# A graph network's gathered rows summed column by column, and handed on in groups of four

## The reference

```
x = x + L0(h)      # per edge: h[src] @ w[type], summed by target
x = x + L1(h)      # three times: mean of the neighbours' rows @ Wl + h @ Wr + b, relu between
x = x + L2(h)      # sums of h_src and of h_src * h_dst by target, @ weight1 and @ weight2, scaled by degrees
x = x + L3(h)      # two graph attentions: scores per edge, softmax by target, weighted sum
```

## Time and profile before

| | us |
|---|---|
| median of 3 runs | 6555.59 |
| span of the profiled execution | 8635.1 |
| PE, DVE, POOL busy in it | 4016.2, 4326.1, 4305.3 |
| layer0: from the first gather to the patch's gather | 731 (3108 to 3839) |
| layer1, layer2, layer3 likewise | 744, 698, 678 |
| att1: from its first gather to its last | 728 (6012 to 6740) |
| granted TensorE clock, mean of the span | 0.650 of full |

### The profile page before, as it was taken

The page is one execution under the profiler, slowest core; times in us unless marked ns, Lnnn a source line. Parts: engine busy times, 40 slices in busy tenths (PEclk is TensorE's granted clock), DMA queues, the critical chain, the costliest instruction groups (busy, mean ns, idle before and its releaser), DMA issues. The chain is left out here.

```text
span 8635.1 us, 76490 instructions
## 1 busy us (share of the span) xinstructions
PE 4016.2 (47%) x19708; PEld 2671.9 (31%) x19708; DVE 4326.1 (50%) x14882; ACT 2282.2 (26%) x5999; POOL 4305.3 (50%) x4026
## 2 busy tenths in 40 slices
PE   1111158312888825654563664342465476567000
PEld 0000034101555514443442443332344355233000
DVE  3010069301999944434432553565244698677553
ACT  0000000001777621110110333354111133799000
POOL 5777720575000046546555674774555100888577
PEclk8555589655999955555555555555666666798555
DMA  1111100000222222222222343343122144555222
GB/s 42 47 46 47 47 19 0 21 1 5 103 113 107 99 70 79 69 73 64 69 68 63 112 128 112 94 139 112 44 68 68 77 161 163 125 146 138 76 82 77
DMA packets 413612, 684.96 MB, mean 79 GB/s; under 512 B 283685, under 2 KB 290444, under 8 KB 407978
## 3 DMA queue, kind: packets, MB, share of 16 engines
q1 hardware_dynamic: 282410, 542.14, 17.7%
q0 software_dynamic: 130944, 140.05, 7.5%
HBM read 310.94 MB, written 373.78 MB: 79 GB/s over the span
## 5 line engine op out<-in xcount | busy, mean ns | idle before, releaser
L711 POOL DMA_INDIRECT G<-states,srcq x1568 | 1678.9, 1071 | 851.1 <-issue 479.5
L1133 DVE TENSOR_TENSOR_SCAN R<-same,R,G 128x28 f32<-128x28 f32 x4480 | 883.8, 265 | 622.1 <-issue 499.9
L1793 PE MATMUL PS<-ident,HH 128*128 128x128 f32 x2357 | 529.8, 376 | 1257.4 <-ACT AT L2063 373.2
L2063 ACT COPY AT<-PS 128x512 f32<-128x512 f32 (+1 forms) x494 | 283.7, 581 | 2467.3 <-remote 1375.1
L1793 PEld LDWEIGHTS PS<-ident,HH 128*128 128x128 f32 x2357 | 402.8, 205 | 1332.9 <-issue 409.9
L711 POOL DMA_INDIRECT EE<-node_info,srcq x392 | 394.4, 1006 | 545.0 <-DMA node_info<-XC 415.7
L1701 PE MATMUL PS<-R 128*128 128x392 f16 x784 | 283.0, 361 | 673.2 <-remote 375.7
L711 POOL DMA_INDIRECT G<-states,srci x392 | 406.7, 1038 | 321.0 <-ACT HH L2161 199.1
L1808 PEld LDWEIGHTS PS<-WD,AT 128*128 128x128 f32 x2358 | 505.8, 316 | 183.0 <-issue 182.7
L1808 PE MATMUL PS<-WD,AT 128*128 128x64 f32 x2358 | 560.6, 416 | 0.0
L824 POOL DMA_INDIRECT out_nodes<-O,dstq x392 | 430.9, 1099 | 188.2 <-issue 123.3
(11 more groups left out here) (412 smaller groups left out, 10157.6 us busy)
## 6 DMA issues: line engine op xcount, KB each, us to landing
states<-O SPq DMA_DIRECT2D x70, 896.0 KB, 3.6
HH<-states SPq DMA_DIRECT2D x56, 896.0 KB
total<-R SPq DMA_DIRECT2D x56, 896.0 KB
XB<-resid SPq DMA_DIRECT2D x42, 896.0 KB
states<-HH SPq DMA_DIRECT2D x28, 896.0 KB, 3.9
G<-states,srcq POOLq DMA_INDIRECT x1568
resid<-XB SPq DMA_DIRECT2D x28, 896.0 KB
xl_of_src<-O SPq DMA_DIRECT2D x14, 1792.0 KB
```

The source lines that it names most:

```text
L711: return pool.indirect_dma_start(to, None, table_, bass.IndirectOffsetOnAxis(ap=idx, axis=0), bounds_check=bound, oob_is_err=False).then_i ...
L1133: last = dve.tensor_tensor_scan(out=out_[:, order, f], data0=flags[:, order], data1=in_[:, order, f], initial=initial[:, f:f + 1], op0=ALU ...
L1793: last = pe.transpose(PS[:, 4 + k, q * P:(q + 1) * P], HH[:, b, (g * G4 + q) * D2:(g * G4 + q + 1) * D2], ident[:])
L2063: act.copy(AT[:, k, 0:n * P], PS[:, 4 + k, 0:n * P]).then_inc(s_copied, 1)
```

## The change

In the four `LAYERS` passes the 64 scans of a chunk are replaced by 28 steps of `scalar_tensor_tensor`, each over the 64 features of one column: column j = column j-1 times the flag `same` plus the gathered column j. Every step waits for the one before. After each four columns the operand of that group is made and `s_ready` is incremented, 7 times a chunk instead of once. The gathers signal one semaphore for each group and buffer (`s_g[b][g]`), and DVE waits for a group at a time. PE's `turn` waits for its own group. In `layer0` and `layer1` the one-hots and their matmuls move ahead of the chunk's rows and products. In `att1` ACT copies the left halves group by group, each copy one group ahead of the products, and PE waits for a group's left halves. A function `first_operands` replaces `operands` in the patch.

```diff
-                def gathered(i, it, b):
+                def rows_of(i, it, b):
                     step.reset()
                     dve.wait_ge(s_tot[b], before[layer, "tot"] + 16 * (it + 1))
                     step(dve.memset(col(SCR), 0.0))
-                    dve.wait_ge(s_g[b], before[layer, "gath"] + 16 * C * (it + 1))
-                    if k == 3:
-                        step(tt(cut(G[:, b, :]), cut(G[:, b, :]), over(rs_src[:, bass.ds(i * C, C)], D), ALU.mult))
-                    scans(cut(R[:, b, 0:CD]), cut(G[:, b, :]), same[:, bass.ds(i * C, C)], R[:, 1 - b, CD - D:CD], D).then_inc(s_scan, 1)
...
+                    for g in range(GROUPS):
+                        dve.wait_ge(s_g[b][g], before[layer, "gath"] + 16 * G4 * (it + 1))
+                        if k == 3:
+                            some = cut(G[:, b, g * G4 * D:(g + 1) * G4 * D])
+                            step(tt(some, some, over(rs_src[:, bass.ds(i * C + g * G4, G4)], D), ALU.mult))
+                        for j in range(g * G4, (g + 1) * G4):
+                            row_before = R[:, b, (j - 1) * D:j * D] if j else R[:, 1 - b, CD - D:CD]
+                            row = dve.scalar_tensor_tensor(out=R[:, b, j * D:(j + 1) * D], in0=row_before, scalar=same[:, bass.ds(i * C + j, 1)],
+                                                           in1=G[:, b, j * D:(j + 1) * D], op0=ALU.mult, op1=ALU.add)
+                            if j < C - 1:
+                                step(row)
+                        if g == GROUPS - 1:
+                            row.then_inc(s_scan, 1)
+                            dve.wait_ge(s_scan, before[layer, "scan"] + 1 + i)
+                        if g == 0:
+                            if k == 3:
+                                dve.wait_ge(s_rscaled, i + 1)
+                            else:
+                                dve.wait_ge(s_ld[b], before[layer, "ld"] + 16 * (it + 1))
+                            step(dve.memset(col(SCR), 0.0))
+                        operands(k, i, b, g).then_inc(s_ready, 1)
...
                     def turn(i, it, b):
-                        gathered(i, it, b)
-                        state(i, it, b)
+                        step.reset()
                         source_hots(i)
+                        rows_of(i, it, b)
...
-                pe.wait_ge(s_ready, before[phase, "ready"] + 1 + i)
+                if phase in LAYERS:
+                    pe.wait_ge(s_ready, before[phase, "ready"] + GROUPS * i + g + 1)
...
+                if phase == "att1":
+                    pe.wait_ge(s_left, GROUPS * i + g + 1)
...
             def scores1(i, it, b):
-                act.wait_ge(s_g[b], before["att1", "gath"] + 16 * C * (it + 1))
-                act.copy(cut(HH[:, b, :], D2)[:, :, 0:D], cut(G[:, b, :])).then_inc(s_left, 1)
-                put_scores(i, it, b)
+                def left(g):
+                    act.wait_ge(s_g[b][g], before["att1", "gath"] + 16 * G4 * (it + 1))
+                    some = slice(g * G4, (g + 1) * G4)
+                    act.copy(cut(HH[:, b, :], D2)[:, some, 0:D], cut(G[:, b, :])[:, some]).then_inc(s_left, 1)
```

## The result

The changed kernel takes 6359.17 us (median of 4 runs, 6354.62 to 6363.26) against 6554.74 us before (4 runs, 6538.55 to 6563.34): a ratio of 0.9706, 95% interval 0.9691 to 0.9720. It is 196 us faster.

What follows compares the result with a forecast made beforehand. POOL's gathers, about 1.30 us each, were taken to bound every pass. Terms -48 (layer0, layer1), -12 (layer2), +7 (layer3) and -12 (att1) sum to -65, so 6555.6 becomes 6490 us, range 6420 to 6600.

Steps and rivals of the forecast that it cites:

- The reading of the disturbed profile: All passes: the plain run has gathers at about 1.30 us; POOL's 338.8 us of waits for scans are no gain.
- Rival (b): Between chunks: POOL's waits for the scans exist in the plain run too; -300 us at most, so 6270; chance 0.12.
- The step that failed: Every pass: 14 x 36.4 us of gathers plus what follows the last gather, everything else moving beside them.
- Rival (d): Columns beside gathers: steps 0.73 us apart, hidden in layer0 to layer2, layer3 +166 us, 6650 in all; chance 0.15.
- Ends of layer0 and layer1: Behind the last gather: 40.3 us becomes 14.5 with nothing uncovered; 24 taken for each layer, -48 us together.
- Layer2: End of layer2: the front of the tail shortens from 16.3 to 4.2 us, the rest stays; -12 us.
- Layer3: New loop through DVE and ACT of 38.5 us a chunk against 36.4 of gathers; +7 us, bounds -15 to +62.
- att1: Start of the first attention: first products go at about 6047 instead of 6059.5; -12 us, bounds -12 to +14.
- The chained steps: DVE's column steps: 0.22 us of work plus a 0.14 us gap for a register or address instruction.
- (a): Gaps between chained steps vanish: layer3 gives -15 us instead of +7, ends another -5; 6462; chance 0.14.
- What was to show it: Profile after: layer0's end 20 us shorter, last group within 5 us, step gaps 0.1 to 0.15, layer3 chunks 38 apart.

Runs made afterwards that it cites:

- e_split: e_none with the operand of layer0 and layer1 made by seven instructions of 256 elements instead of one of 1792: 6511.54 us, ratio to before 0.9932.
- e_whole: Changed kernel, but layer0 and layer1 make the operand once a chunk, by one 1792-element instruction behind the 28 columns: 6435.70 us.
- e_res2: Changed kernel with layer2's residual addition (1792 elements) made by seven instructions of 256: 6362.22 us.
- e_none: Kernel before with only the gather semaphores changed, 14 instead of 2: 6535.68 us, ratio 0.9976.
- e_four: Kernel before with four gather semaphores (two for each buffer, 14 columns each) instead of two: 6532.91 us, one run.
- e_shift: Kernel before, two gather semaphores kept, with three more small memsets on POOL ahead of the first pass: 6541.05 us, one run.
- the second profile: Kernel before, unchanged, profiled once more, this time without the first profile's 2079 us extra; its phases are 530.5, 533.9, 539.0, 567.1 and 551.0 us.

## Why the prediction was wrong, point by point

**The reading of the disturbed profile** was right: the plain run has gathers every 1.30 us, POOL waits for no scan, and the 338.8 us of the earlier trace rows were no money to earn. Rival (b), which had them real, gave 6270. That the measured 6359 lies nearer to this than to the forecast is luck: its mechanism is in no undisturbed profile. What disturbed the first one is open.

**The step that failed** is the sentence that a pass is 14 x 36.4 us plus its end, with all DVE work beside it for nothing. Measured without the disturbance, the stretches from first gather to last were 21 (layer0), 21 (layer1), 26 (layer2), 53 (layer3) and 36 us (att1) longer than 392 x 1.30, for two reasons that the sum had at nought:

- DVE's instructions of 1792 elements hold a gather, one a chunk in layer0 and layer1, two in layer2, four in layer3. The change cuts those of the operand and of the scaling into sevenths: -12.4, -12.6, -2.1 and -27.4 us of gathers in layer0 to layer3, 54.5 in all. (att1, whose DVE instructions stay as they were, has -3.7, which is within the 5.7 us by which its gathers differ between the kernels that share its changed code.) e_split, e_whole and e_res2 show it in both directions. Layer2 gained so little because the residual additions left in it now meet a gather nearer to their own start: the 12 gathers that they hold take 2.37 us in the median, and took 1.63 before.
- Two gather semaphores cost POOL 5 us a phase in idle times of 2 us: 26 us. e_none, e_four and e_shift show it. Nothing in the part of the change that was priced could have told it. The disturbed profile has a wait at the same gathers too, but of 0.9 to 1.0 us in layer0 to layer2, beside waits of 3 to 28 us.

**The rule that was weighed the wrong way.** Rival (d) named the Trainium skill, "SBUF — State Buffer", section "Who interferes with whom": a DVE instruction with two SBUF inputs contends with a GpSimd instruction that reads SBUF, and the second to issue blocks fully. The prediction asked it only of the columns and scans, as a price of the change, and put it aside because 62 scans take 0.185 us each beside gathers. They do: an instruction of 0.2 us holds nobody for long. But the rule speaks of the whole length of an instruction, so it had to be asked of every one of 2.02 us, which the change takes away. The rows hold one of these (L1305) too. The trace agrees with the page for gathers, which read their indices from SBUF (`idx`): one issued during such an instruction ends 0.87 us after it. The other direction does not show here: in the second profile, from layer0 to att1, 101 of 126 such instructions begin while a gather runs, and all 126 take 2.0 to 2.1 us; a gather under way already takes 1.00.

**Ends of layer0 and layer1**: predicted 40.3 to about 16, -24 each; measured -29.5 and -29.7. DVE's part was 12.1 and is 11.6. PE's was sized 24.0 to 10.1 and is 32.1 to 10.3: the earlier trace rows came from a stretch in which PE began at the higher clock (granted clock 0.97; eight transposes in 1.04 us, 0.13 each), and in the undisturbed run they take 0.24 each (twelve in 2.90, clock 0.50). The 24.0 was the mis-sized term, by 8 us. The 10.1 were right by luck: the 1.0 in them, put down as one group's transposes, is the time of two groups at the higher clock, and at 0.50 one group takes 1.11. (Its terms add to 14.3, not 14.5, which changes nothing here.) The store came into the open with 4.1 us, the full amount that the prediction allowed.

**Layer2**: -12 predicted at the end, -15.3 measured. **Layer3**: the loop was put at 38.5 us and is 38.1 (3549.10 to 3587.22, the two residual additions), so the mechanism is there: DVE waits for ACT's scaled rows in it,

```profile
3567.66 0.06 DVE L1358 MEMSET cols<- 128x1 f32 x1 [8.35 <-ACT HH L2115]
```

and that wait ends 11.9 us after the statistics, where 13.5 was put, while six groups take 18.3 instead of 17.2. By this the sum had +7 against "530". The mistake stands on the other side of the comparison: before, a chunk of layer3 took 40.2 us and the pass 563 to its last gather, not 14 x 36.4. The end is 13.3 shorter. So -46 instead of +7, the largest miss of the sum. **att1**: -12 predicted at the start of the stage; it came at its end, 15.8 us from the last gather to sum1's first transposes, where ACT's copy of 1.68 us and seven groups had stood behind the last gather, and now one group does:

```profile
4708.52 1.68 ACT L2161 COPY HH<-G 128x1792 f32<-128x1792 f32 x1 [12.62 <-DMA G<-states,srci]
```
```profile
4526.34 0.40 ACT L2174 COPY HH<-G 128x256 f32<-128x256 f32 x1 [3.65 <-DMA G<-states,srci]
```

(before, and after). **The chained steps** were put 0.36 us apart, with 0.25 and 0.50 as bounds: 0.22 for the step and a gap of 0.14, 0.03 or 0.28. Of the changed kernel, DVE in a loop of layer3, and in layer2's last chunk, which stands outside the loop:

```profile
3557.74 0.28 DVE L1346 SCALAR_TENSOR_TENSOR R<-R,same,G 128x64 f32<-128x64 f32 x1
3558.17 1.15 DVE L1346 SCALAR_TENSOR_TENSOR R<-R,same,G 128x64 f32<-128x64 f32 x3 [0.15 <-DVE R L1346]
```
```profile
3328.72 1.24 DVE L1346 SCALAR_TENSOR_TENSOR R<-R,same,G 128x64 f32<-128x64 f32 x4 [1.29 <-DMA G<-states,srcq]
```

The steps start 0.43 us apart in the loop and 0.32 outside ((1.24 - 0.28) / 3). So the gap of the forecast is right, 0.15 with an address from a register, and 0.04, near the 0.03 of (a), is found only outside the loops. The step was mis-sized: 0.28 us, where the 0.22 was that of a `tensor_tensor` of 64 elements.

**What was to show it.** The end of layer0 shrank by more than 20 (29.5), DVE's last group was done 3.7 us after the last gather, the gap between two column steps is 0.15 us, and layer3's chunks start 38 us apart: right. Slower columns beside gathers (d), and the loop beyond 43.5 us, did not come.

## What to carry to other kernels

Where an engine is called the bound because it is busy without a break, look at the length of each of its instructions, not only at the gaps: 54.5 us were won on gathers that took 1.6 to 2.9 us instead of 1.00, each of them beside one particular DVE instruction. Work "hidden" under gathers on POOL is only free if its instructions with two SBUF inputs are short; cutting them costs DVE time and gives POOL more, until DVE's own loop is the longer one, as in layer3. And a disturbed profile gives the order of events, but its clock and its durations beside the disturbance are no prices.

## What the runs showed of the hardware

- A gather issued while a DVE instruction with two SBUF inputs of 1792 elements (2.02 us) runs ends 0.87 us after it; in the five phases it takes up to 2.9 us instead of 1.00. Beside scans of 28 elements and steps of 64 it takes 1.00, beside the batch-norm statistics (one input, 3.65 us in a row) 1.00 too, and 1.00 also beside a reduction with one input and the same 2.02 us. DVE's own instruction takes no longer for meeting a gather.
- With two semaphores for the gathers of a pass POOL stops for 2 us once in 112 gathers; with four or fourteen it does not. Why is open.
- A DVE step `scalar_tensor_tensor` of 64 elements takes 0.28 us, and chained ones start 0.43 us apart with an address from a register, in a loop, and 0.32 without, outside the loops.
- sum1, in which no kernel differs, took from its first transposes to its carries 427 to 429 us in the changed kernel (twice), the kernel before and the same with three memsets more, and 437 to 444 in the other twelve, with a granted clock of 0.66 to 0.67 or 0.63 to 0.65 over the stage. What sets it is open, and it hid 8 to 17 us in the total times of those twelve.
